# Eleven projections in a feed-forward, its normalisation moved to ScalarE, and two pairs of attention scores interleaved

## The chip, the cores and the metric

The kernel runs on one core of a Trainium2 chip. The metric is the device time of one execution in microseconds (us). The engines are named TensorE (PE; PEld is its weight load), VectorE (DVE), ScalarE (ACT), GpSimd (POOL) and SyncE (SP).

## The reference, cut to what matters

Eight items of 512 tokens with 256 channels pass through two layers. What the change touches:

```
# layer 0, branch "ffn" (two depths), for each item
h = shift_token(x)                    # second half of the channels one token later
x = x + local_attention(h) @ wo       # window 128, 8 heads
h = shift_token(x)
h = (h - mean(h)) / sqrt(var(h) + 1e-5) * lg + lb
a, g = split(h @ w1 + b1)             # 682 columns each
x = x + (a * gelu(g)) @ w2 + b2
# layer 1, branch "attn": causal latent attention, 16 heads, scores over 24 of 32 rows
# layer 1, branch "ffn": 8 experts, the best 2 of each token; rows are scattered to experts
```

Beside the feed-forward branch of depth 0, layer 0 has a retention branch for the same item.

## The kernel before, in words

The program is a chain of stages k = -1 to 15, written out by hand for every engine. Stages 0 to 7 are the items at depth 0, each beside the retention of the same item; I call them retention stages. Stages 8 to 15 are the items at depth 1, each beside the latent attention (item b = k - 8). In stages 9 to 15 the second half of the latent attention of item b - 1 is also done ("behind"); stage 15 is the last one and has no next item. After it comes the loop over 71 expert tiles.

A stage has three parts. First a loop over four token tiles t: the q/k product (four matmuls) and the v product (two) of the next item, the retention or latent work between them, and on VectorE and GpSimd the rotary parts (L1655, L1657), their sum (L1497), the sums of squares (L1661) and the power (L1501). Then the loop over the feed-forward's chunks c = 0 to 5. Then a loop over u with the local attention of the next item.

PSUM is used as two rings of four banks of 512 columns. Ring A is emptied mostly by ScalarE, ring D by VectorE. The names that take two banks are q/k, its transposes, the scores and a few more. A product waits until the jobs that were last in its banks are emptied; the order of the jobs is written out in ring_a_jobs and ring_d_jobs, and every engine works through its instructions in that order.

The feed-forward: shifted_stats (L1631, L1633) takes mean and variance of each tile of the shifted input, which SyncE puts together by small DMAs (L566 to L570). GpSimd makes rs, the power -1/2 (L1466). shifted_apply on VectorE runs ln_apply (L1641) in eight instructions of 128x128 at t = 1 (in the last stage t = 2). TensorE turns z (L733), ScalarE applies lg and lb (norm_in, L1254). Chunks are 120 hidden columns wide, the last 82. up_projection makes the gate half in ring A and the value half in ring D (L722), gelu empties the first (L1281), gate_up multiplies (L1717), and down_projection sums over six chunks.

Latent scores: a pair of heads w has three rounds r (ROUNDS): 512, 512 and 256 columns for each head, two banks each. latent_scores issues a pair's heads in two groups of 32 rows (L878). clipped moves each round to the space of the pair on VectorE (L1775), latent_exp (L1307) runs on ScalarE when all three are there, and causal (L1513, L1514, L1516) masks on GpSimd. latent_values of group g (L888) waits for the masks of pairs 2g and 2g + 1. by_token turns the result on TensorE (L896) and scales it on VectorE.

At the end of the last stage, counts of rows for each expert are known. SyncE writes rows of zeros behind each expert's region (zero_rows, L627), four before the table is ready and four after the first weights (L643), then waits for all scatters and zeros, and gathers the first rows (L650).

## Time and profile before

| | us |
|---|---|
| three runs, median (lowest, highest) | 2849.97 (2844.25, 2851.5) |
| profiled execution, its own time | 2849.19 |
| its span | 2847.4 |
| TensorE busy | 2703.8 |
| VectorE, ScalarE, GpSimd busy | 1546.2, 1235.8, 1051.0 |

The span is that from the first to the last instruction. Matmuls are pipelined and their ends are modelled, so the pitch from one group to the next tells more than the busy time of one. A time in square brackets behind a row is how long the engine had been idle, with what ended it.

### The profile page before, as it was taken

How to read it: one execution, taken by the hardware profiler on the slowest of the kernel's cores; microseconds unless marked ns; L12 is line 12 of the kernel's file. 1: busy time of each engine (PE TensorE's matmuls, PEld its weight loads, DVE VectorE, ACT ScalarE, POOL GpSimd, SP SyncE). 2: the span in 40 equal slices, each digit the busy share in tenths (PEclk: the TensorE clock that was granted, in tenths of full speed). 3: DMA queues.
4: the chain of work that ended last, by engine and by line, in shares of the span. 5: the costliest groups of instructions: out<-in, count | busy, mean ns of one | idle time of the engine just before them, and what ended most of it. 6: DMA issues, size and time to landing. Idle time of an engine off the chain costs nothing.

```text
span 2847.4 us, 41985 instructions
## 1 busy us (share of the span) xinstructions
PE 2703.8 (95%) x15582; PEld 1833.3 (64%) x15582; DVE 1546.2 (54%) x3730; ACT 1235.8 (43%) x2287; POOL 1051.0 (37%) x726
## 2 busy tenths in 40 slices
PE   6999999999999999999999999999997799999993
PEld 4575757566575757555555555555564578999993
DVE  6565566575666555677676767576855322100004
ACT  4454444545453444545454545454543234222222
POOL 5434243443434243445454536363623122111110
PEclk9999999999999999999999999999998899999997
DMA  4000000000001001101010101010000666899987
GB/s 143 12 16 26 26 16 30 27 27 16 26 16 57 18 24 52 61 5 53 4 53 5 53 4 45 12 39 19 30 34 23 235 247 250 304 365 365 360 334 243
DMA packets 85907, 261.83 MB, mean 92 GB/s; under 512 B 10668, under 2 KB 49916, under 8 KB 67020
## 3 DMA queue, kind: packets, MB, share of 16 engines
q1 hardware_dynamic: 75004, 237.19, 23.0%
q0 software_dynamic: 6480, 17.77, 1.7%
q10 hardware_dynamic: 4224, 4.19, 0.4%
q8 instruction: 128, 2.10, 0.3%
q14 instruction: 71, 0.58, 0.1%
HBM read 210.81 MB, written 44.11 MB: 90 GB/s over the span
## 4 chain that ended last, share of the span: by engine, by line
PE 65%; issue 13%; DVE 10%; POOL 6%; ACT 3%; DMA 2%; SPq 0%; POOLq 0%; DVEq 0%; ACTq 0%
PE s_pD L722 19%; PE s_pA L722 18%; PE s_pD L878 5%; PE s_pA L772 3%; PE s_pD L794 3%; PE s_pA L781 3%; PE s_pA L1167 2%; PE s_pD L1182 2%; POOL acc_s L1598 2%; DVE s_qk L1676 2%; POOL s_rinv L1501 2%; PE s_pA L761 1%; DMA s_z<-s_cur 1%; PE s_pA L733 1%; PE s_pA L888 1%
## 5 line engine op out<-in xcount | busy, mean ns | idle before, releaser
L1507 POOL TENSOR_TENSOR s_qk<-s_qk,s_rrec 128x1024 f32<-128x1024 f32 (+1 forms) x128 | 220.7, 1725 | 502.7 <-DVE s_rrec L1682 502.5
L722 PE MATMUL s_pA<-s_w_wqkv,s_curT 128*128 128x512 f32 x768 | 354.6, 602 | 5.6 <-ACT s_curT L1212 3.7
L1236 ACT ACTIVATE s_qk<-s_qk,s_mx 128x256 f32<-128x256 f32 (+1 forms) x512 | 239.8, 471 | 95.3 <-DVE s_mx L1676 95.3
L1775 DVE TENSOR_SCALAR s_pairs<-s_pD 128x1024 f32<-128x1024 f32 (+1 forms) x192 | 195.0, 1040 | 151.4 <-PE s_pD L878 150.1
L722 PEld LDWEIGHTS s_pA<-s_w_wqkv,s_curT 128*128 128x128 f32 x768 | 142.6, 191 | 176.7 <-issue 163.2
L1501 POOL TENSOR_TENSOR s_rinv<-s_ssq,s_half 128x16 f32<-128x16 f32 x64 | 230.1, 3596 | 59.5 <-DVE s_ssq L1661 59.5
L1598 POOL DMA_INDIRECT acc_s<-s_w_w,s_sq x71 | 68.5, 964 | 470.7 <-ACT s_w_w L1444 463.5
L2139 DVE COPY s_w_wo<-s_pD 128x256 f32<-128x256 f32 x71 | 29.9, 421 | 338.5 <-PE s_pD L1153 338.5
L1466 POOL TENSOR_TENSOR s_rs<-s_ve,s_half 128x4 f32<-128x4 f32 x40 | 42.0, 1050 | 433.4 <-DVE s_ve L1636 433.3
L878 PE MATMUL s_pD<-s_mixer 32*128 32x512 f32 (+3 forms) x1024 | 180.7, 467 | 11.9 <-DVE s_pairs L1775 9.0
L722 PE MATMUL s_pA<-s_zT,s_w_w 128*120 128x512 f32 (+1 forms) x384 | 183.8, 601 | 4.2 <-ACT s_pairs L1281 3.1
L1676 DVE CUSTOM_DVE_ANT_0 s_qk<-s_pA,s_maskw 128x256 f32<-128x256 f32 (+1 forms) x512 | 167.9, 386 | 25.3 <-PE s_pA L772 24.8
L722 PE MATMUL s_pD<-s_zT,s_w_w 128*120 128x512 f32 (+1 forms) x384 | 180.7, 593 | 0.0
L1497 POOL TENSOR_TENSOR s_qk<-s_qk,s_rot 128x1024 f32<-128x1024 f32 x64 | 151.1, 2361 | 51.8 <-DVE s_qk L1657 51.8
L1307 ACT ACTIVATE s_pairs<-s_pairs 128x2560 f32<-128x2560 f32 x64 | 149.7, 2339 | 44.2 <-DVE s_pairs L1775 44.0
L1218 ACT COPY s_qk<-s_pA 128x1024 f32<-128x1024 f32 x64 | 64.8, 1012 | 231.6 <-PE s_pA L722 231.6
L878 PEld LDWEIGHTS s_pD<-s_mixer 32*128 32x128 f32 x1024 | 89.3, 188 | 100.3 <-issue 50.6
L772 PE MATMUL s_pA<-s_qkT 64*128 64x256 f32 (+1 forms) x1024 | 134.2, 380 | 5.7 <-DVE s_mx L1676 3.8
L781 PE MATMUL s_pA<-s_ident,s_qk 128*128 128x128 f32 x896 | 126.9, 282 | 11.4 <-POOL s_qk L1507 6.5
L1665 DVE SCALAR_TENSOR_TENSOR s_qk<-s_rinv,s_qk 128x1024 f32<-128x1024 f32 x64 | 110.9, 1733 | 42.0 <-POOL s_rinv L1501 42.0
L722 PEld LDWEIGHTS s_pD<-s_zT,s_w_w 128*120 128x120 f32 (+1 forms) x384 | 68.6, 179 | 97.1 <-issue 93.1
L1444 ACT ACTIVATE s_w_w<-s_pD,s_w_w 128x256 f32<-128x256 f32 x71 | 33.6, 473 | 219.2 <-PE s_pD L1182 219.2
(268 smaller groups left out, 5724.6 us busy)
## 6 DMA issues: line engine op xcount, KB each, us to landing
s_qkT<-in_m_w SPq DMA_DIRECT2D x48, 1024.0 KB, 6.7
s_v_tm<-in_m_w SPq DMA_DIRECT2D x24, 1024.0 KB, 7.4
s_rot<-in_m_w SPq DMA_DIRECT2D x24, 1024.0 KB, 6.3
s_w_wqkv<-in_m_w SPq DMA_DIRECT2D x23, 1024.0 KB, 7.7
s_qk<-in_m_w SPq DMA_DIRECT2D x23, 1024.0 KB, 5.7
s_w_w<-rows_s SPq DMA_DIRECT2D x71, 129.0 KB, 6.0
s_cur<-in_x SPq DMA_DIRECT2D x8, 512.0 KB, 3.5
xn_s<-s_cur SPq DMA_DIRECT2D x8, 512.0 KB, 2.6
```

The costliest lines, as they stand in the source:

```text
L722: last = nc.tensor.matmul(out, lhs(c), rhs(c), start=(c == 0), stop=(c == n - 1))
L772: last = nc.tensor.matmul(ps[:, place(i) * 256 + lo * P:(place(i) + 1) * 256], qkT[r, h // 2, tile_cols(t)], qkT[r, 4 + h // 2, (t - 1 + l ...
L781: last = nc.tensor.transpose(ps[:, (2 * i + k) * P:(2 * i + k + 1) * P], prob[w % 3][:, i * 256 + k * P:i * 256 + (k + 1) * P], ident[:])
L878: last = nc.tensor.matmul(ps[:, 512 * i + col:512 * i + col + T - kt * P], KT[rows, g % 2, tile_cols(kt)], QT[rows, g % 2, kt * P:T], star ...
L1236: last = nc.scalar.activation(pi, pi, ACT.Exp, scale=-1.0, bias=mx[:, u, i:i + 1], accum_out=rsum[:, u, i:i + 1])
L1307: nc.scalar.activation(ph, ph, ACT.Exp, scale=1.0 / SQ24).then_inc(lexp, 1)
L1497: nc.gpsimd.tensor_tensor(qk[:, t, :], qk[:, t, :], rot[:, t % 2, :], ALU.add)
L1501: nc.gpsimd.tensor_tensor(rinv[:, t, :], ssq[:, t, :], half[:], ALU.pow).then_inc(rinv_rdy, 1)
L1507: nc.gpsimd.tensor_tensor(pi, pi, rrec[:, u, :].unsqueeze(2).broadcast_to((P, 4, 256 - lo)), ALU.mult).then_inc(p_rdy, 1)
L1598: nc.gpsimd.indirect_dma_start(out=S["acc"], out_offset=bass.IndirectOffsetOnAxis(ap=goal[:, w % NX:w % NX + 1], axis=0), in_=m_y[:, w % N ...
L1676: last = nc.vector.tensor_tensor_reduce(out=prob[u % 3][:, h], in0=ps[:, h], in1=maskw[:, lo:256], scale=-1.0, scalar=3e38, op0=ALU.add, o ...
L1775: nc.vector.tensor_scalar(Pl[:, w % SLOTS, :, ROUND_AT[r]:ROUND_AT[r] + ROUND_N[r]], ps[:, :, 0:ROUND_N[r]], 80.0, -80.0, ALU.min, ALU.max ...
```

## The change

1. The feed-forward's 682 hidden columns are split into 42 + 5 x 128 instead of 5 x 120 + 82. The small chunk is now the first. Its value half and its gate half (from column 64 on) stand side by side in w1, so one projection of 106 columns in ring D makes both; the job in ring A falls away. GELU of chunk 0 reads ring D. The memset for the row of ones moves from chunk 5 to chunk 0.
2. The normalisation of the shifted input: VectorE makes shift = -mean * rs in one small instruction, and ScalarE applies scale and shift in eight, after its copies of t = 1.
3. In stages 9 to 14 the scores of pairs 4 and 5 are issued by four_scores, round by round for both pairs, in four groups of 32 rows: round 0 before the q/k product of tile 0, round 1 before its v product, round 2 at tile 1. The clips, exponentials and masks follow in a new order.
4. The zeros for experts 4 to 7 are written from ScalarE's queue in the last stage instead of SyncE's.

```diff
-HCH = 120
+HCH = 128
-HSZ = [min(HCH, HID - HCH * c) for c in range(NHC)]
+HSZ = [HID - HCH * (NHC - 1)] + [HCH] * (NHC - 1)
+GATE = 64
...
 def up_projection(b, c):
-    ps = slotA("g", b, c)
-    project(ps[0:n, 0:T], ... HID + c * HCH ...).then_inc(mmA, 1)
+    n = HCH if c else GATE + HSZ[0]
+    if c:
+        ps = slotA("g", b, c)
+        project(ps, ...).then_inc(mmA, 1)
     ps = slotD("a", b, c)
...
+def four_scores(b, g, r):
+    pe.wait_ge(outD, doneD["lq", b, g])
+    ps = [slotD("sc", b, 2 * g + pr, r) for pr in range(2)]
+    last = {}
+    for kt, col in ROUNDS[r]:
+        for h in range(4):
+            rows = slice(32 * h, 32 * h + 32)
+            i = h % 2
+            last[h] = nc.tensor.matmul(ps[h // 2][:, 512 * i + col:512 * i + col + T - kt * P], KT[rows, g % 2, tile_cols(kt)],
+                                       QT[rows, g % 2, kt * P:T], start=True, stop=True)
+    last[1].then_inc(mmD, 1)
+    last[3].then_inc(mmD, 1)
...
 # TensorE, loop over t
-    if s.behind and t < 3:
+    if s.behind and (s.last and t < 3 or t == 2):
         latent_scores(b - 1, 4 + t, (0, 1))
+    if s.behind and not s.last and t < 2:
+        four_scores(b - 1, 2, 2 * t)
     if s.ahead:
         qk_product(k + 1, t)
...
-    if s.behind and t < 3:
+    if s.behind and (s.last and t < 3 or t == 2):
         latent_scores(b - 1, 4 + t, (2,))
+    if s.behind and not s.last and t == 0:
+        four_scores(b - 1, 2, 1)
     if s.ahead:
         v_product(k + 1, t)
...
 # ScalarE
+def shifted_norm(b):
+    act.wait_ge(shift_h, b + 1)
+    for t in range(NT):
+        for i, ap in enumerate((cur[b % 2][:, t, 0:P], hB[:, t, :])):
+            last = nc.scalar.activation(z[:, t, i * P:(i + 1) * P], ap, ACT.Identity, bias=shift[:, t:t + 1], scale=rs[:, t:t + 1])
+        last.then_inc(norm_h, 1)
...
+    if s.here and t == 1:
+        shifted_norm(k)
-    if s.behind and t < 2:
+    if s.last and t < 2:
         latent_exp(b - 1, 4 + t)
+    if s.behind and not s.last and t in (1, 2):
+        latent_exp(b - 1, 3 + t)
...
+    if s.last and u == 5:
+        act.wait_ge(zero_rdy, 2)
+        act.wait_ge(weight_rdy, TOPK * LAST + 1)
+        for e in range(E // 2, E):
+            n = act.value_load(counts_i[0:1, e:e + 1], min_val=0, max_val=B * T)
+            act.dma_start(S["rows"][bass.ds(n + e * REG, P), :], zrows).then_inc(zero_in, 16)
...
 # GpSimd, ahead of rotary_sum and head_norms of tile t
-    if s.behind and t < (2 if s.last else 3):
+    if s.last and t < 2:
         causal(b - 1, 4 + t)
+    if s.behind and not s.last and t:
+        causal(b - 1, 3 + t)
...
 # VectorE
 def shifted_apply(b):
     dve.wait_ge(rstd_h, b + 1)
-    for t in range(NT):
-        ln_apply(t, halves(b, t), z, norm_h)
+    nc.vector.scalar_tensor_tensor(out=shift[:], in0=mv[:, :, 0], scalar=-1.0, in1=rs[:], op0=ALU.mult, op1=ALU.mult).then_inc(shift_h, 1)
...
+    if s.behind and not s.last and t < 2:
+        clipped(b - 1, 4, (2 * t,))
+        clipped(b - 1, 5, (2 * t,))
     if s.here and t == 0:
         shifted_stats(k, range(0, 2) if s.last else range(0, NT))
...
+    if s.behind and not s.last and t == 0:
+        clipped(b - 1, 4, (1,))
+        clipped(b - 1, 5, (1,))
```

## Rows read from the trace of the kernel before

**Rows 1.** The page, part 1: busy time of each engine.
```profile
PE 2703.8 (95%) x15582; PEld 1833.3 (64%) x15582; DVE 1546.2 (54%) x3730; ACT 1235.8 (43%) x2287; POOL 1051.0 (37%) x726
```

**Rows 2.** Groups by line (busy us, mean ns, idle before), a half of the normalisation.
```profile
L1641 DVE SCALAR_TENSOR_TENSOR s_z<-s_z,s_mv,s_rs 128x128 f32<-128x128 f32 x64 | 23.7, 371 | 0.0
```

**Rows 3.** Timeline (start us, us) of retention stage 4.
```profile
626.10 0.34 DVE L1641 SCALAR_TENSOR_TENSOR s_z<-s_cur,s_mv,s_rs 128x128 f32<-128x128 f32 x1
...
628.32 1.01 ACT L1218 COPY s_qk<-s_pA 128x1024 f32<-128x1024 f32 x1 [6.30 <-PE s_pA L722]
...
650.47 1.88 PE L722 MATMUL s_pA<-s_zT,s_w_w 128*120 128x512 f32 x4
...
653.90 1.04 PE L761 MATMUL s_pA<-s_ident,s_qk 128*128 128x128 f32 x8
```

**Rows 4.** Timeline of latent stage 12, scores of pairs 4 and 5.
```profile
1686.82 1.99 PE L878 MATMUL s_pD<-s_mixer 32*128 32x512 f32 x12
...
1688.07 2.36 DVE L1775 TENSOR_SCALAR s_pairs<-s_pD 128x1024 f32<-128x1024 f32 x2 [2.15 <-PE s_pD L878]
...
1688.75 3.70 PE L722 MATMUL s_pA<-s_w_wqkv,s_curT 128*128 128x512 f32 x8
...
1692.38 0.70 PE L878 MATMUL s_pD<-s_mixer 32*128 32x256 f32 x4
...
1695.48 0.29 DVE L1631 BATCH_NORM_STATS2 s_stat<-s_cur 128x6 f32<-128x128 f32 x1 [2.35 <-DMA s_z<-s_cur]
...
1696.32 3.15 DVE L1775 TENSOR_SCALAR s_pairs<-s_pD 128x512 f32<-128x512 f32 x3
...
1704.22 0.60 PE L896 MATMUL s_pD<-s_ident,s_mixer 128*128 128x128 f32 x4
```

**Rows 5.** Timeline of latent stage 12, from the exponential of pair 5 on.
```profile
1704.90 2.34 ACT L1307 ACTIVATE s_pairs<-s_pairs 128x2560 f32<-128x2560 f32 x1
...
1710.59 1.73 POOL L1516 TENSOR_TENSOR s_pairs<-s_pairs,s_tri 128x512 f32<-128x512 f32 x1
...
1714.20 2.35 POOL L1497 TENSOR_TENSOR s_qk<-s_qk,s_rot 128x1024 f32<-128x1024 f32 x1 [1.89 <-DVE s_qk L1657]
...
1716.51 3.90 POOL L1501 TENSOR_TENSOR s_rinv<-s_ssq,s_half 128x16 f32<-128x16 f32 x1
...
1719.00 2.36 PE L888 MATMUL s_pA<-s_pairs,s_mixer 128*32 128x512 f32 x32
...
1740.83 2.36 PE L888 MATMUL s_pA<-s_pairs,s_mixer 128*32 128x512 f32 x32 [0.65 <-POOL s_pairs L1516]
...
1743.58 1.41 DVE L1717 SCALAR_TENSOR_TENSOR s_pairs<-s_pD,s_w_b,s_pairs 120x512 f32<-120x512 f32 x2
...
1745.17 1.98 PE L722 MATMUL s_pA<-s_zT,s_w_w 128*120 128x512 f32 x4 [0.51 <-ACT s_pairs L1281]
```

**Rows 6.** Instructions of line L1294 (ns min/median/max), a normalisation ScalarE already does.
```profile
L1294 ACT ACTIVATE s_mixer<-s_mixer,s_shift,s_rs x28: 585/587/602, 1195.7 to 2069.9; 128x256 f32<-128x256 f32 x28
```

**Rows 7.** Windows: stretch, busy of PE, PEld, DVE, ACT, POOL, granted clock, DMA.
```profile
1190.00:1195.00 5.00, 2.61 (x24) 1.87 (x24) 4.68 (x14) 2.90 (x9) 1.28 (x3) 1.00 0.58 208
1195.00:1200.00 5.00, 4.24 (x19) 3.39 (x20) 2.73 (x16) 4.28 (x13) 3.76 (x4) 0.51 0.01 3
```

**Rows 8.** Timeline of TensorE: stage 8 (two places) and stage 15.
```profile
1141.94 0.67 PE L722 MATMUL s_pA<-s_w_wqkv,s_curT 128*128 128x512 f32 x1 [0.36 <-ACT s_sq L1221]
...
1195.76 1.65 PE L772 MATMUL s_pA<-s_qkT 64*128 64x256 f32 x6 [3.15 <-DVE s_mx L1676]
...
2150.33 3.77 PE L722 MATMUL s_pA<-s_zT,s_w_w 128*120 128x512 f32 x4 [1.11 <-ACT s_zT L1254]
```

**Rows 9.** Timeline of the queues of SyncE and GpSimd before the expert tiles.
```profile
2223.25 4.29 SPq L627 DMA_DIRECT2D rows_s<-s_w_fC  x4
2223.53 0.96 POOL L1527 DMA_INDIRECT rows_s<-s_w_w,s_rows_i  x1 [0.30 <-issue]
...
2232.87 0.36 SPq L650 DMA_DIRECT2D s_w_w<-rows_s  x1
```

More of the change, by code:

```diff
@@ L26 @@
 HID = 682
-HCH = 120
+HCH = 128
 NHC = 6
-HSZ = [min(HCH, HID - HCH * c) for c in range(NHC)]
+HSZ = [HID - HCH * (NHC - 1)] + [HCH] * (NHC - 1)
+HAT = [0] + [HSZ[0] + HCH * c for c in range(NHC - 1)]
+GATE = 64
+ONES = 32
+UPW = GATE + HSZ[0] + 2 * HCH * (NHC - 1)
 LH, LDH, LDR, LAT = 16, 16, 8, 64
@@ L119, in ring_a_jobs @@
         for c in range(NHC):
-            if s.here:
+            if s.here and c:
                 j += [("g", k, c)]
@@ L170, in ring_d_jobs @@
         for t in range(NT):
-            if s.behind and t < 3:
+            if s.behind and (s.last and t < 3 or t == 2):
                 j += pair(b - 1, 4 + t)
+            if s.behind and not s.last and t < 2:
+                j += [("sc", b - 1, 4 + i, r) for r in ((0, 1) if t == 0 else (2,)) for i in range(2)]
             if s.ret:
@@ L624, in _ @@
             sp.dma_start(S["rows"][E * REG:E * REG + P, :], zrows).then_inc(zero_in, 16)
-            def zero_rows(e):
+            for e in range(E // 2):
                 n = sp.value_load(counts_i[0:1, e:e + 1], min_val=0, max_val=B * T)
                 sp.dma_start(S["rows"][bass.ds(n + e * REG, P), :], zrows).then_inc(zero_in, 16)
-            for e in range(E // 2):
-                zero_rows(e)
             sp.wait_ge(table, 1)
@@ L644, in fetch @@
                 if u == 0:
-                    for z in range(E // 2, E):
-                        zero_rows(z)
                     for k in range(TOPK):
@@ L1004, in _ @@
                         ret_products(k, t)
-                    if s.behind and t < 3:
+                    if s.behind and (s.last and t < 3 or t == 2):
                         latent_scores(b - 1, 4 + t, (2,))
+                    if s.behind and not s.last and t == 0:
+                        four_scores(b - 1, 2, 1)
                     if s.ahead:
@@ L1277, in gelu @@
                 n = HSZ[c]
-                ps = takeA("g", b, c)
+                at = 0 if c else GATE
+                if c:
+                    ps = takeA("g", b, c)
+                else:
+                    act.wait_ge(mmD, DJ["a", b, 0] + 1)
+                    ps = pD[:, colsD[DJ["a", b, 0]]]
                 if b > 0 or c >= 2:
                     act.wait_ge(outD, doneD["a", b, c - 2] if c >= 2 else doneD["a", b - 1, NHC - 1])
-                nc.scalar.activation(gl_of(b)[c % 2][0:n], ps[0:n, 0:T], ACT.Gelu, bias=W["b1"][0:n, 1, c:c + 1]).then_inc(outA, 1)
+                last = nc.scalar.activation(gl_of(b)[c % 2][0:n], ps[at:at + n, 0:T], ACT.Gelu, bias=W["b1"][at:at + n, 1, c:c + 1])
+                last.then_inc(outA if c else first_gelu, 1)
             def final_tanh(b, i):
@@ L1970, in _ @@
                 for t in range(NT):
-                    if s.behind and t < 3:
+                    if s.behind and (s.last and t < 3 or t == 2):
                         clipped(b - 1, 4 + t, (0, 1))
+                    if s.behind and not s.last and t < 2:
+                        clipped(b - 1, 4, (2 * t,))
+                        clipped(b - 1, 5, (2 * t,))
                     if s.here and t == 0:
@@ L1979, in _ @@
                         ret_rotary(k, t)
-                    if s.behind and t < 3:
+                    if s.behind and (s.last and t < 3 or t == 2):
                         clipped(b - 1, 4 + t, (2,))
+                    if s.behind and not s.last and t == 0:
+                        clipped(b - 1, 4, (1,))
+                        clipped(b - 1, 5, (1,))
                     if s.past and t == 1:
@@ L2217, in arrange @@
     r["w_ln"] = np.stack([np.stack([per(g), per(b)], 1) for g, b in zip(a["L0_ffn_ln_g"], a["L0_ffn_ln_b"])], 1)
-    r["w_w1"] = np.stack([ch(w) for w in a["L0_ffn_w1"]], 1)
+    up = []
+    for c in range(NHC):
+        value = a["L0_ffn_w1"][:, :, HAT[c]:HAT[c] + HSZ[c]]
+        gate = a["L0_ffn_w1"][:, :, HID + HAT[c]:HID + HAT[c] + HSZ[c]]
+        room = np.zeros(value.shape[:2] + (0 if c else GATE - HSZ[0],), np.float32)
+        up += [value, room, gate]
+    r["w_w1"] = np.stack([ch(w) for w in np.concatenate(up, 2)], 1)
     b1 = np.zeros((HCH, DEPTH, 2, NHC), np.float32)
@@ L2224, in arrange @@
             for i in range(2):
[L2225 to L2227 removed]
+                at = 0 if c or not i else GATE
+                b1[at:at + n, l, i, c] = a["L0_ffn_b1"][l, i * HID + HAT[c]:i * HID + HAT[c] + n]
+            w2[0:n, l, c] = a["L0_ffn_w2"][l, HAT[c]:HAT[c] + n]
+        w2[HSZ[0], l, 0] = a["L0_ffn_b2"][l]
     r["w_b1"], r["w_w2"] = b1, w2
```

23 lines of the change are left out of this document (12 added, 11 removed).

## The prediction

> **What bounds the kernel now.** I read the busy times first, then the groups by line, then the timeline of one stage of each kind. The reader is to see in the first which engine is full, in the second what the moved instructions cost where they are, and in the last which wait ends last. TensorE is busy for 2703.8 of 2847.4 us [rows 1]; in the retention stages (0 to 7) it hardly ever waits, and each of the latent stages 9 to 14 holds a few waits of at most 1 us. So an instruction taken off TensorE is worth its own pitch, as long as no other engine moves into its place; work taken off VectorE is worth nothing unless TensorE waited for it.
>
> **The feed-forward in eleven projections.** Each of the twelve 512-column projections of an item is two matmuls, which the trace shows as four records [rows 3]. The gate and value projections of chunk 0 fill TensorE from 650.47 to 653.90, so one costs 1.72 us [rows 3]. The width of a chunk (120, 82 or now 128 columns of weights) does not show in that pitch, and the down projection keeps its six chunks. Taken out once in each item: -1.72 us. In the eight retention stages nothing waits for it, since VectorE idles there before its first product: 8 x 1.72 = -13.8 us. The memset that moves to chunk 0 (0.5 us, VectorE) and the later first GELU lie inside that idle time.
>
> **The normalisation on ScalarE.** VectorE loses eight instructions of about 0.34 us an item and keeps one small one [rows 2]. ScalarE gains eight. The nearest row is its own 128x256 Identity with scale and bias by row, 585 ns [rows 6]; at half the columns I take 0.38 us each, 3.0 us for eight (bounds 2.4 and 4.0). They stand after the copies of t=1, so everything behind them on ScalarE waits until VectorE reaches its step. In a retention stage VectorE gets there at 626.10 and the next copy starts at 628.32 [rows 3]: it would be 1 us late, which the retention branch's projections between two uses of those banks cover. I cost it at nothing; without that cover it is the 1.1 us of stage 8. In stage 8 that cover is gone, and TensorE already waits 0.36 us for the square behind the copy [rows 8]: +1.1, which leaves -0.6 for that stage.
>
> **The scores of pairs 4 and 5, stages 9 to 14.** This decides. Now the first two rounds of pair 4 take 1.93 us (1686.82 to 1688.75) and its third 0.63; two row groups run side by side [rows 4]. With four side by side, both pairs need 1.06 + 1.06 + 0.65 = 2.8 us instead of twice 2.56. But a round then fills all four banks of the D ring, so the next round needs both clips before it. VectorE's order is: both clips of round 0, the statistics of all four tiles, both clips of round 1. The last tile's statistics wait for a DMA until 1695.48 whatever TensorE does, and the first clip after them starts at 1696.32 [rows 4]. Two clips take 2.36 (1688.07), so these end at 1698.7. By my count TensorE has done round 0, q/k product, round 1 and v product at 1694.5, and waits 4.3 us. Then 0.65 + 3.64 + 1.85 us bring it to the turn by token at 1704.95; before, that began at 1704.22 [rows 4]. The whole saving in the scores is gone: +0.7 us at this point (bounds: -2.3 if the statistics end early enough, +1.5).
>
> The Trainium skill, TensorEngine Tiling (Array Packing), section PSUM Bottleneck, says that tiling speeds up TensorE but not the emptying of PSUM, which may become the limit after a fourfold speed-up. The trace agrees as far as it goes: two clips of together 2.36 us do not fit beside a v product of 1.85, so by that rule alone, without the DMA, the third round would wait 0.5 us and not 4.3, and 1.8 us of the gain would be left.
>
> **What is late next.** The exponential of pair 5 began at 1704.90 before, that of pair 4 one tile earlier [rows 5]. Now ScalarE first waits for the shift, which VectorE makes only after the turn by token (about 1706.5), spends 3.0 us on the rows, and then takes 2.34 for pair 4: 1711.9. GpSimd's order now puts the mask of pair 5 behind the rotary sum and the power of tile 1: mask 4 (three instructions that end with the row at 1710.59, 2.65 to 3.1 us), sum 2.35, power 3.9, mask 5 again 2.65 [rows 5]. That ends at 1723.5. TensorE would want the values of that group at about 1720.4 (it did at 1719.00 before [rows 5]): a second wait of some 3.1 us, +4.5 in all against before (bounds +2.5 and +5.5). The copy of q/k tile 2 behind the exponential costs 0.5 of this.
>
> After that TensorE saves its 1.72, and it had waits of 0.65 and 0.51 us of its own (1740.83, 1745.17), which can absorb some of the rest: +1.6 there if TensorE is the limit. But the gate product that frees the GELU (1743.58) hangs on VectorE's clips of pair 7, the rotary parts of tile 3, GpSimd's power and the router's chain, all behind the same wait: +4.1 if they are the limit [rows 5]. I take +3.1 a stage. The shorter queue on VectorE is in this.
>
> **The clock.** A gap of 3.15 us before 1195.76 [rows 8] is followed by five microseconds at 0.51 of the clock, and then more [rows 7]: the lower level, 1.2 GHz. It means for four records of a projection 3.77 us (at 2150.33) instead of 1.88 [rows 8, 3]. So a wait of 4.3 us is likely to cost a stretch at half rate, and one of 3.1 us may. A dense stretch of 3.4 to 6.8 us at half rate loses 1.7 to 3.4 us. I take 2.5 for both waits of a stage together (bounds 0 and 6.8, two stretches of each size). The Trainium skill, TensorE: Matmul & The Clock Gate, section Why this matters for your kernels, warns of the same: a pause between bursts of matmuls brings back the lower rate.
>
> Latent stages: 6 x (3.1 + 2.5) = +33.6 us.
>
> **The last stage and the turn to the experts.** In stage 15 the normalisation itself may get faster, but exponential 5 now stands between it and the copies, so I count nothing for it. The projection that is removed ran at the half clock (3.77 us [rows 8]) and the next at nearly the full one: between 1.72 and 3.4, I take -2.4. At the end SyncE issued four rows of zeros from 2223.25 for 4.3 us after the first weights; the first gather, on which TensorE waits, went out at 2232.87 [rows 9]. Moved to ScalarE, they go out before those weights; behind them on ScalarE stand only two copies whose products TensorE can make while it waits. What is late next is the last scatter, issued at 2223.53 by GpSimd [rows 9] and, as I estimate, landed by 2230: -2.8 (bounds 0 and -4).
>
> **The sum.** -13.8 - 0.6 - 2.4 - 2.8 = -19.6; with +33.6 it is +14.0. The profiled execution took 2849.2 us (span 2847.4 and 1.8 around it), 0.8 below the median of the three runs. That gives 2863. About 0.3%, 8.5 us, is what a measurement of this kernel can tell from no change.
>
> **The rivals.**
> - The gain arrives (0.27): VectorE's statistics and the masks are not what TensorE meets, for instance because the values of the group come late enough for GpSimd, and only the first wait is left. The place is the turn by token and the values behind it. A stage then ends at +0.7 + 0.5 - 1.72 = -0.5; 6 x -0.5 - 19.6 = -22.6: 2827. It decides from the point where mask 5 ends before TensorE wants it, 3.1 us earlier than I count. For it: rows of GpSimd's power differ by up to 1 us, and the ScalarE time is estimated. Against it: four instructions in series on one engine, each with its row.
> - The waits come but the clock holds (0.22): 6 x 3.1 - 19.6 = -1.0: 2848. For it: gaps of 1 to 2 us elsewhere leave the clock at 1.00. Against it: the first wait is longer than the gap of 3.15 us.
> - The four row groups do not run side by side (0.09): the change would not do what it says. No row shows four of them. A round of both pairs takes 1.93 instead of 1.06, mostly out of the first wait, and the third 0.4 more; the first wait shrinks to 2.6 us and the clock probably holds: 6 x 3.5 - 19.6 = +1.4: 2851.
> - Both waits bring long stretches at half rate (0.07): 6 x (3.1 + 6.8) - 19.6 = +39.8: 2889.
>
> The forecast has 0.35. Cases of both signs hold most of the chance; the forecast's own range is 2855 to 2874, by the bounds of the two waits. The whole range, 2824 to 2879, reaches to the rival that gains and leaves out the worst clock. Slower by over 0.3%: the forecast's 0.35 less a little, the long half rates and a tenth of the others: 0.46. Within: 0.25. Faster: 0.29.
>
> **What would show it.** In a latent stage of the changed kernel: TensorE idle some 4 us before the third round, ended by the clip L1775; some 3 us before the values (L888), ended by GpSimd's mask L1516; granted clock near 0.5 after them. Row groups: four records of round 0 starting together, and 1.06 us for its eight. Retention stages shorter by 1.7 us each. The first gather 3 us nearer to the table. Latent stages no longer than before would prove the forecast wrong; retention stages that do not shrink would take its other half.

## The result, and the profile after

The changed kernel takes 2892.81 us (median of 4 runs, 2891.88 to 2893.25) against 2850.73 (4 runs, 2844.25 to 2852.95) in the same session: 1.015 of the time before, 95% interval 1.0136 to 1.0164. It is 42 us slower; the forecast was 2863 with a range to 2879. The profiled execution has a span of 2890.1 against 2847.4 us.

The head of its profile page, which answers to [rows 1]:

```profile
span 2890.1 us, 41880 instructions
PE 2705.3 (94%) x15518; PEld 1817.5 (63%) x15518; DVE 1488.9 (52%) x3618; ACT 1287.8 (45%) x2415; POOL 1032.9 (36%) x726
```

TensorE has 64 fewer matmul records (two for each of 32 matmuls) and yet is busy for 1.5 us longer; VectorE lost 57 us of work. Neither says where the time went. For that I cut both traces at the first addition of each stage (L1695 before, L1742 after) and compared lengths. What each stage gained (-) or lost (+), us, by this cut:

| stage | 0 to 7 | 8 | 9 | 10 | 11 | 12 | 13 | 14 | 15 to the end |
|---|---|---|---|---|---|---|---|---|---|
| after - before | -0.5 each | +2.6 | +7.2 | +8.4 | +9.5 | +5.7 | +9.5 | +7.7 | -3.5 |

Before stage 0 it is -0.3. The latent stages 9 to 14 hold +48.0. Windows of the changed kernel over stages 4, 8 and 12 (PEclk is the mean granted clock):

```profile
core 0: us, PE busy (x) PEld busy (x) DVE busy (x) ACT busy (x) POOL busy (x), PEclk, DMA share, GB/s
600.77:729.51 128.74, 127.93 (x686) 81.86 (x684) 77.48 (x194) 63.86 (x136) 49.83 (x27) 1.00 0.07 23
1112.82:1242.28 129.46, 122.40 (x637) 76.28 (x636) 74.81 (x168) 65.43 (x129) 51.78 (x32) 0.96 0.11 37
1703.45:1855.68 152.23, 140.23 (x813) 82.25 (x812) 97.63 (x226) 78.30 (x137) 69.84 (x51) 0.98 0.08 27
```

Stage 12, TensorE's timeline where the forecast had its two waits (compare [rows 4, 5]):

```profile
1710.14 1.14 PE L895 MATMUL s_pD<-s_mixer 32*128 32x512 f32 x8
1711.21 3.70 PE L725 MATMUL s_pA<-s_w_wqkv,s_curT 128*128 128x512 f32 x8
1714.85 1.15 PE L895 MATMUL s_pD<-s_mixer 32*128 32x384 f32 x16
1715.92 1.98 PE L725 MATMUL s_pA<-s_w_wqkv,s_curT 128*128 128x512 f32 x4
1722.29 0.71 PE L895 MATMUL s_pD<-s_mixer 32*128 32x256 f32 x8 [4.39 <-DVE s_pairs L1823]
1722.94 7.11 PE L725 MATMUL s_pA<-s_w_wqkv,s_curT 128*128 128x512 f32 x12
...
1750.20 4.05 PE L906 MATMUL s_pA<-s_pairs,s_mixer 128*32 128x512 f32 x32 [5.13 <-POOL s_pairs L1561]
```

Three things are to be seen. The four row groups work: round 0 of both pairs, four matmuls of 512 columns in eight records, takes 1.07 us to the next start (1710.14 to 1711.21), where one pair's first two rounds took 1.93. Then TensorE waits 4.39 us for clips and 5.13 us for mask 5; all six latent stages have both waits, 4.39 to 4.45 and 5.12 to 5.13. And behind each wait the work is slow: the twelve records from 1722.94 take 7.11 us instead of 5.4, in part in a stretch at 1.2 GHz (granted clock 0.51):

```profile
1722.90:1726.30 3.40, 3.40 (x8) 1.51 (x5) 3.16 (x5) 0.00 (x0) 0.00 (x0) 0.51 0.01 2
```

VectorE in the first wait: the clips of round 1 (L1823) start when the statistics of the last tile are done, and these waited for a DMA.

```profile
1718.95 0.29 DVE L1678 BATCH_NORM_STATS2 s_stat<-s_cur 128x6 f32<-128x128 f32 x1 [2.35 <-DMA s_z<-s_cur]
...
1719.79 2.35 DVE L1823 TENSOR_SCALAR s_pairs<-s_pD 128x1024 f32<-128x1024 f32 x2
```

ScalarE (first two rows) and GpSimd in the second wait, which answers to [rows 5]: the last of eight norms, exponential 4, mask 4, sum, power, mask 5.

```profile
1734.07 0.48 ACT L1277 ACTIVATE s_z<-s_z,s_shift,s_rs 128x128 f32<-128x128 f32 x1
1734.45 2.32 ACT L1342 ACTIVATE s_pairs<-s_pairs 128x2560 f32<-128x2560 f32 x1
```

```profile
1736.85 0.73 POOL L1558 TENSOR_TENSOR s_pairs<-s_pairs,s_tri 128x256 f32<-128x256 f32 x1 [4.70 <-ACT s_pairs L1342]
...
1738.22 2.26 POOL L1561 TENSOR_TENSOR s_pairs<-s_pairs,s_tri 128x512 f32<-128x512 f32 x1
1740.45 2.80 POOL L1542 TENSOR_TENSOR s_qk<-s_qk,s_rot 128x1024 f32<-128x1024 f32 x1
1743.21 3.36 POOL L1546 TENSOR_TENSOR s_rinv<-s_ssq,s_half 128x16 f32<-128x16 f32 x1
1746.54 0.72 POOL L1558 TENSOR_TENSOR s_pairs<-s_pairs,s_tri 128x256 f32<-128x256 f32 x1
1747.22 1.70 POOL L1559 TENSOR_TENSOR s_pairs<-s_pairs,s_tri 128x256 f32<-128x256 f32 x1
1748.89 1.25 POOL L1561 TENSOR_TENSOR s_pairs<-s_pairs,s_tri 128x512 f32<-128x512 f32 x1
```

Retention stage 4: the merged projection is there, and the down projection has grown. Each of its two groups begins with records of 43 rows. Before, the two groups took 5.38 and 5.19 us; now 5.88 (672.48 to 678.36) and 5.87:

```profile
671.48 1.16 PE L775 MATMUL s_pA<-s_qkT 64*128 64x128 f32 x16
...
672.48 1.68 PE L725 MATMUL s_pD<-s_w_w,s_pairs 43*128 43x256 f32 x6
...
678.36 1.13 PE L775 MATMUL s_pA<-s_qkT 64*128 64x256 f32 x8
679.42 0.65 PE L784 MATMUL s_pA<-s_ident,s_qk 128*128 128x128 f32 x4
680.01 1.76 PE L725 MATMUL s_pD<-s_w_w,s_pairs 43*128 43x256 f32 x6
...
685.88 1.04 PE L736 MATMUL s_pA<-s_ident,s_z 128*128 128x128 f32 x8
```

Summed over both kernels' matmul rows and clock records, the mean latent stage comes out so: TensorE idle 12.4 us instead of 4.6 (+7.8); busy at the half rate 8.7 us instead of 2.3, which costs half of the difference (+3.2); work saved, 2.3 us of scores and 0.5 in the feed-forward (-2.8). That is +8.2, and +8.0 was measured.

Not every stretch at the half rate follows a wait. The kernel before has one of 3.4 us late in four of its six latent stages, and in the 8 us before each TensorE never pauses for more than 0.4 us. In its stage 12 the granted clock is 1.00 while TensorE is busy for all of 7.40 us, the last part with products of 8 columns and of 64 rows, and then 0.50:

```profile
1785.00:1792.40 7.40, 7.40 (x35) 5.03 (x35) 3.05 (x6) 2.18 (x8) 0.00 (x0) 1.00 0.00 0
1792.50:1795.80 3.30, 3.30 (x15) 2.71 (x13) 1.29 (x2) 0.58 (x1) 0.00 (x0) 0.50 0.00 0
```

In the changed kernel one of these four is left. So the stretches at the two waits cost more than the net +3.2: about 4.1 us a stage, less 0.9 for those that are gone.

### The profile page after: what moved, and what is told of

It reads as the page before. It is cut to its first block, busy times and chain, and to the rows that moved or that the text cites. A ratio compares the mean times of both kernels' runs of the same rounds, so it can differ in the third digit from the quotient of the medians.

```text
span 2890.1 us, 41880 instructions
## 1 busy us (share of the span) xinstructions
PE 2705.3 (94%) x15518; PEld 1817.5 (63%) x15518; DVE 1488.9 (52%) x3618; ACT 1287.8 (45%) x2415; POOL 1032.9 (36%) x726
## 4 chain that ended last, share of the span: by engine, by line
PE 61%; issue 14%; DVE 10%; POOL 7%; ACT 4%; DMA 3%; SPq 0%; ACTq 0%; POOLq 0%; DVEq 0%
PE s_pD L725 19%; PE s_pA L725 15%; PE s_pD L883 4%; PE s_pA L775 3%; PE s_pA L784 3%; PE s_pD L797 3%; PE s_pA L1189 2%; PE s_pA L906 2%; PE s_pD L1204 2%; POOL acc_s L1645 2%; POOL s_rinv L1546 1%; DMA s_z<-s_cur 1%; POOL rows_s L1572 1%; PE s_pA L764 1%; DVE s_pairs L1823 1%
## 5 line engine op out<-in xcount | busy, mean ns | idle before, releaser
L725 PE MATMUL s_pA<-s_w_wqkv,s_curT 128*128 128x512 f32 x768 | 366.9, 619 | 7.9 <-ACT s_curT L1234 3.7
L1823 DVE TENSOR_SCALAR s_pairs<-s_pD 128x1024 f32<-128x1024 f32 (+1 forms) x192 | 194.6, 1042 | 204.2 <-PE s_pD L883 182.8
L1546 POOL TENSOR_TENSOR s_rinv<-s_ssq,s_half 128x16 f32<-128x16 f32 x64 | 216.5, 3382 | 86.0 <-DVE s_ssq L1708 86.0
L725 PE MATMUL s_pD<-s_zT,s_w_w 128*128 128x512 f32 (+1 forms) x384 | 182.4, 598 | 2.9 <-ACT s_zT L1283 2.9
L725 PE MATMUL s_pA<-s_zT,s_w_w 128*128 128x512 f32 x320 | 152.4, 599 | 3.1 <-ACT s_pairs L1315 3.1
L883 PE MATMUL s_pD<-s_mixer 32*128 32x256 f32 (+3 forms) x832 | 146.6, 467 | 6.0 <-DVE s_pairs L1823 3.1
L775 PE MATMUL s_pA<-s_qkT 64*128 64x256 f32 (+1 forms) x1024 | 132.3, 378 | 7.4 <-DVE s_mx L1723 3.6
L725 PE MATMUL s_pD<-s_w_w,s_pairs 43*128 43x256 f32 x480 | 137.7, 401 | 0.0
L784 PE MATMUL s_pA<-s_ident,s_qk 128*128 128x128 f32 x896 | 125.8, 280 | 3.5 <-POOL s_qk L1552 2.8
L725 PEld LDWEIGHTS s_pD<-s_zT,s_w_w 128*128 128x128 f32 (+1 forms) x384 | 71.2, 188 | 88.9 <-issue 83.1
```

The lines of the kernel that those rows point to most:

```text
L725: last = nc.tensor.matmul(out, lhs(c), rhs(c), start=(c == 0), stop=(c == n - 1))
L775: last = nc.tensor.matmul(ps[:, place(i) * 256 + lo * P:(place(i) + 1) * 256], qkT[r, h // 2, tile_cols(t)], qkT[r, 4 + h // 2, (t - 1 + l ...
L784: last = nc.tensor.transpose(ps[:, (2 * i + k) * P:(2 * i + k + 1) * P], prob[w % 3][:, i * 256 + k * P:i * 256 + (k + 1) * P], ident[:])
L883: last = nc.tensor.matmul(ps[:, 512 * i + col:512 * i + col + T - kt * P], KT[rows, g % 2, tile_cols(kt)], QT[rows, g % 2, kt * P:T], star ...
L1546: nc.gpsimd.tensor_tensor(rinv[:, t, :], ssq[:, t, :], half[:], ALU.pow).then_inc(rinv_rdy, 1)
L1823: nc.vector.tensor_scalar(Pl[:, w % SLOTS, :, ROUND_AT[r]:ROUND_AT[r] + ROUND_N[r]], ps[:, :, 0:ROUND_N[r]], 80.0, -80.0, ALU.min, ALU.max ...
```

## The experiments

Eighteen kernels ran, sixteen of them timed against the kernel before. The median of the kernel before moved between 2844 and 2851 us from session to session, so ratios are what is compared; across sessions I trust them to about 0.2%, since the changed kernel's 2892.81 came beside 2850.73 and a kernel with stages as long as its own (64 rows, below) took 2892.97 beside 2844.66. "After" is the changed kernel.

**Undoing or mending one part of the change.** The first gives the scores of pairs 4 and 5 their old order on every engine; the second:

```diff
-                rows = [HSZ[c] + (c == 0) for c in range(NHC)]
+                rows = [65 if c == 0 else HCH for c in range(NHC)]
```

The third puts ln_apply back on VectorE. The fourth, on VectorE:

```diff
                         clipped(b - 1, 5, (2 * t,))
+                    if s.behind and not s.last and t == 0:
+                        clipped(b - 1, 4, (1,))
+                        clipped(b - 1, 5, (1,))
                     if s.here and t == 0:
                         shifted_stats(...)
```

> The changed kernel with the score products of pairs 4 and 5 in the order of before on all engines (clips, exponentials and masks with them); merge, norm on ScalarE and zero rows kept. If the two waits of stages 9 to 14 (4.4 and 5.1 us each) with the half-rate stretches behind them are made by the new order of the scores: those six stages lose nearly all of their +48 us, about 2847 (2842 to 2855). If the norm on ScalarE makes the second wait by itself: only the first wait goes, about 2868. If the norm costs the latent stages a little (1 us each) through ScalarE: 2853.

> The changed kernel with chunk 0 of the down projection's sum taken over 65 rows (rows 43 to 64 of the weights are zero) in place of 43; nothing else. If the 43-row products run in a 64-row form of the array and the change of form within each of the four sums costs the 1.2 us by which the two groups of L725 in the down projection grew: groups back at 5.4 and 5.2 us, about 1.2 a stage, sixteen items, 2893 - 19 = 2874 (2866 to 2880). If the growth has another cause (order of the chunks, the buffer's arrival): no change, 2893, or slightly more for a second fill of ones.

> The changed kernel with the shifted input's normalisation back on VectorE, everything else kept. If eight norms ahead of exponential 4 on ScalarE (3.1 us) carry the second wait: it falls from 5.1 to about 2.5 us, stage 8 gives back its +2.6, VectorE pays 0.4 to 0.6 x 8 ahead of its clips; with the clock's stretch in half of the stages 2893 - 20 = 2873 (2862 to 2885). If the place of mask 5 behind sum and power on GpSimd sets that wait alone, and VectorE's norm delays the same chain by as much: 2890 (2887 to 2898).

> The changed kernel with VectorE's two clips of round 1 put ahead of the four tiles' statistics, which wait for transfers; nothing else moved. If the first wait (4.4 us) is these clips held behind the statistics: it falls under 1 us in stages 9 to 14, six times 3.5 to 6 us with the half-rate stretch, 2893 - 25 = 2868 (2858 to 2876). If TensorE's next work waits for the statistics or for the stretch at half rate anyway: under 8 us, 2885 or more.

| run | us | ratio to before (95%) | stage 4 | stage 8 | stages 9 to 14, sum |
|---|---|---|---|---|---|
| after | 2892.81 | 1.015 (1.0136 to 1.0164) | -0.5 | +2.6 | +48.0 |
| scores undone | 2852.69 | 1.0036 (1.0022 to 1.005) | -0.5 | -1.2 | +7.3 |
| 65 rows | 2879.74 | 1.0123 (1.0107 to 1.0138) | -1.7 | +0.6 | +49.0 |
| norm on VectorE | 2883.54 | 1.0146 (1.0131 to 1.0162) | -0.5 | +0.3 | +38.0 |
| clips first | 2870.31 | 1.0091 (1.0076 to 1.0107) | -0.5 | -0.3 | +27.4 |

(The last three columns are stage lengths against the kernel before, from one profile each.) By these profiles the order of the scores made 41 of the 48 us. That is its upper end: the profiled execution of the first run is the fastest of its five (2847.14, median 2852.69), and by the ratios undoing the scores gives back 1.1%, 32 us. The clips alone made the first wait: with them in front it falls from 4.4 to 0.69, and 20.6 us go from these stages. The second wait stays, 5.12:

```profile
1705.49 0.71 PE L895 MATMUL s_pD<-s_mixer 32*128 32x256 f32 x8 [0.69 <-DVE s_pairs L1823]
...
1733.45 4.49 PE L906 MATMUL s_pA<-s_pairs,s_mixer 128*32 128x512 f32 x32 [5.12 <-POOL s_pairs L1561]
```

The norm on ScalarE made 1.7 us of the second wait (3.44 without it) and 2.4 of stage 8's loss. By its ratio the run is hardly faster than after, 1.0146 against 1.015: its profiled execution (span 2877.9) is one of its fastest (timed runs 2879.6 to 2889.41), so the stage sums of that row flatter it.

In the retention stages the 65 rows give back what was missing: every undisturbed one is 1.70 shorter than before, the 1.72 of the forecast. The latent stages gain nothing from them (+49.0 against +48.0): TensorE is idle there for 13.7 us in the mean stage instead of 12.4, so the 1.2 us saved became waiting, and the whole run gained 8 us by the ratios and 13 by the medians, where 19 were expected. The same two groups in stage 4, now 5.38 and 5.18 us:

```profile
666.94 1.16 PE L775 MATMUL s_pA<-s_qkT 64*128 64x128 f32 x16
668.04 1.56 PE L725 MATMUL s_pD<-s_w_w,s_pairs 65*128 65x256 f32 x6
...
673.42 1.14 PE L775 MATMUL s_pA<-s_qkT 64*128 64x256 f32 x8
674.48 0.66 PE L784 MATMUL s_pA<-s_ident,s_qk 128*128 128x128 f32 x4
...
680.16 1.04 PE L736 MATMUL s_pA<-s_ident,s_z 128*128 128x128 f32 x8
```

**Why 43 rows cost 1.2 us.** Two looks. One takes 64 rows. The other keeps 43 and turns the order of the first sum of each group, so that its 43-row chunk comes last and stands beside the 43-row chunk of the second sum:

```diff
+                    at = lambda c: c if k else (c + 1) % NHC
```

> The changed kernel with 64 rows instead of 43 in chunk 0 of the down projection (65 rows gave retention stages of 127.6 us, 43 rows 128.7). If the cost goes with a form of the array for 64 rows or fewer: 128.7. If it goes with the number of rows, 64 and 65 are alike: 127.6.

> The changed kernel (43 rows, chunk 0 first in each sum) with one difference: in the first of the two sums of a group the chunk of 43 rows is taken last, so that it stands next to the 43-row chunk of the second sum. If each change between row counts costs time, the changes in a group fall from four to two and half of the 1.2 us comes back: retention stages 128.1 instead of 128.7 (127.6 with 65 rows). If a 43-row product is slow by itself, wherever it stands: 128.7 as in the changed kernel.

Stage 4 of the run with 64 rows and of the one with 65:

```profile
600.77:729.52 128.75, 127.93 (x686) 81.88 (x684) 77.55 (x193) 63.68 (x136) 49.83 (x27) 1.00 0.07 23
```

```profile
596.24:723.81 127.57, 126.76 (x686) 82.39 (x684) 78.02 (x194) 63.71 (x136) 49.81 (x27) 1.00 0.07 24
```

With 64 rows the stage is as long as with 43 (128.74), with 65 it is 1.18 shorter: the step lies between 64 and 65, and below it the number of rows does not matter. I call the two sides forms of the array. With the order turned the stage takes 128.34, a gain of 0.40 where I expected 0.6 and the rival 0. The rows show why:

```profile
669.74 1.16 PE L775 MATMUL s_pA<-s_qkT 64*128 64x128 f32 x16
...
676.60 1.13 PE L775 MATMUL s_pA<-s_qkT 64*128 64x256 f32 x8
677.66 0.66 PE L784 MATMUL s_pA<-s_ident,s_qk 128*128 128x128 f32 x4
...
683.73 1.04 PE L736 MATMUL s_pA<-s_ident,s_z 128*128 128x128 f32 x8
```

I had not counted the neighbours. The first group stands between products of 64 rows (L775), the second between products of 128 (L784, L736). Count each change between 64 rows or fewer and more, from neighbour to neighbour. First group: 2 with 65 rows, 4 in after, 4 with the order turned. From the start of L775 to the start of the next L775 it takes 6.48, 6.88 and 6.86 us. Second group: 0, 4 and 2 changes; from L784 to L736 5.68, 6.46 and 6.07. Four differences, +0.40 and +0.38 for two more changes, +0.39 for two, +0.78 for four: 0.2 us a change, whatever stands between them. The Trainium skill, TensorEngine Tiling (Array Packing), section Key Properties, says that a change of the tiling mode drains TensorE. The trace agrees, and gives the price here.

**The mended order, and what is left without it.** The next four build on these. The first has clips, exponentials and masks of pairs 4 and 5 in a mended order, with the norm on ScalarE and 43 rows as in after. On ScalarE:

```diff
+                    if s.behind and not s.last and t == 1:
+                        latent_exp(b - 1, 4)
+                        latent_exp(b - 1, 5)
                     if s.here and t == 1:
                         shifted_norm(k)
```

> The changed kernel with four row groups kept but its order mended: VectorE clips round 1 ahead of the statistics, ScalarE takes exponentials 4 and 5 ahead of the eight norms, GpSimd masks 4 and 5 ahead of sum and power of token tile 1, mask 6 stays at tile 3. If the second wait (5.1 us, still there with the clips alone moved) is exponential 4 behind the norms plus mask 5 behind sum and power: it is gone or under 1 us, six times 5.1 plus about 2 for the half-rate stretch behind it below the run with the clips alone (2870): 2870 - 40 = 2830 (2824 to 2842), and the interleaving then gains. If it comes from GpSimd's masks being slow beside VectorE in any order: 2855 to 2868.

> The changed kernel with the scores in the order of before and the normalisation on VectorE, and 65 rows in chunk 0 of the down projection: what is left is the merge and the zero rows. The merge's 1.7 us in the eight retention stages and stage 8 (15.3), about 0.7 in each latent stage (4) and 3.4 behind stage 15: 2844 - 23 = 2821 (2815 to 2828). If the norm on VectorE is what holds the latent stages up: above 2830.

> As the run before it, but with the normalisation kept on ScalarE. The difference of the two is the norm's move alone. If it is free or a small gain, as forecast (stage 8 -0.6, none elsewhere): 2820 (2814 to 2826). If ScalarE is what holds TensorE in the latent stages (its copies of q and k come 3 us late and bring half-rate stretches, as the medians of the run with the scores undone hint, 9 us above before): 2832 (2827 to 2840).

> The changed kernel whole (four row groups, norm on ScalarE, merge, zero rows) with the mended order and 65 rows in chunk 0. If merge and order add up: 1.2 us in each of sixteen stages below the run with the mended order, 2830 - 15 = 2815 (2808 to 2828). If the latent stages hide the merge: 2822.

| run | us | ratio (95%) | stages 9 to 14 |
|---|---|---|---|
| mended order | 2851.8 | 1.0023 (1.0014 to 1.0032) | +9.8 |
| old scores, norm on VectorE, 65 rows | 2838.89 | 0.9979 (0.997 to 0.9988) | +8.4 |
| old scores, norm on ScalarE, 65 rows | 2841.71 | 0.9992 (0.9983 to 1.0001) | +14.0 |
| mended order, norm on ScalarE, 65 rows | 2843.03 | 0.9991 (0.9982 to 1) | +10.8 |

Both waits go, as forecast. Yet none of the four times came in: each was expected 18 to 28 us lower. In the second run, of what the change saves only the retention stages' 1.7 us and the last stage's part arrive; the latent stages are 1.4 us longer than before though they have 1.7 us less to do. In its stage 12 TensorE waits 0.77 us for VectorE's product of chunk 0 and 1.09 for mask 7. In the mended order it does not wait for mask 7 at all, but there is a third wait, for the clips of pair 7, before the merged projection:

```profile
1699.55 0.71 PE L895 MATMUL s_pD<-s_mixer 32*128 32x256 f32 x8 [0.69 <-DVE s_pairs L1827]
...
1715.78 5.39 PE L725 MATMUL s_pA<-s_w_wqkv,s_curT 128*128 128x512 f32 x12 [0.47 <-ACT s_sq L1243]
1730.95 2.96 PE L725 MATMUL s_pD<-s_zT,s_w_w 128*106 128x512 f32 x4 [3.56 <-DVE s_pairs L1827]
```

**Where the latent stages' savings go.** First suspicion: the merged projection goes to ring D, and the gate projection in ring A that used to stand in front covered the clips. I moved the small chunk to third place, with old scores, with four row groups, and with those and the norm on ScalarE.

> Old scores, norm on VectorE, 65 rows, zero rows moved, and the small merged chunk in third place instead of first. With it first, the latent stages gave the merge's 1.7 us back: two new gaps of 0.8 to 1.7 us (before the second value projection, behind VectorE's product of chunk 0, which now waits for a GELU that starts only after the merged projection) and 1.0 before the values of group 3. If the place of the chunk makes them: they go, the latent stages gain 1.5 to 2.5 us each against the run with the chunk first, 2839 - 12 = 2827 (2821 to 2832). If the latent stages are bound by another chain (VectorE and GpSimd into mask 7) that no chunk's place touches: 2836 to 2840.

> As the run before it, with four row groups in the mended order. With the chunk first the mended order had a third wait of 3.6 us before the merged projection, for the clips of pair 7 that free its bank. With a gate projection (the other ring) first, 1.7 us of it are covered: 2843 - 6 x 2 - some of the clock = 2829 (2822 to 2836). If the saved time in the scores (2.3 us a stage) reaches the end at all, it is below the run before it; if VectorE's chain to the clips of pair 7 is the limit, it is level or slower by up to 8.

> As the run before it with the normalisation on ScalarE. VectorE's 3 us of norms a stage are ahead of the clips of pair 7 in the run before it; if those clips are the limit, this is faster by 1 to 2 us a stage: 2829 - 9 = 2820. If ScalarE's wait for the shift holds the copies of q and k by as much: level or up to 4 slower, as with the scores in the old order (2841.7 against 2838.9).

Measured 2842.31 (0.9983, 0.9975 to 0.9992), 2841.05 (0.9981, 0.9972 to 0.999) and 2851.66 (1.0018, 1.001 to 1.0027). The suspicion falls: where the gaps were they go or shrink (the third wait, 3.56 us, to 1.46), and they come back before the values of group 3, 1.74 us in stage 12 of the first and 2.71 in the second, both ended by GpSimd's mask. The third run against the second is the norm alone: 0.4% slower, the opposite of what I expected there. A window of the second, from the first sum on GpSimd to mask 7 in stage 12:

```profile
1690.87:1729.82 38.95, 33.94 (x144) 15.79 (x140) 35.84 (x41) 24.27 (x24) 38.95 (x20) 1.00 0.00 1
```

GpSimd is busy for all of the 38.95 us and VectorE for 35.84. TensorE, at 33.94, is no longer what bounds this part. Part of that busy time is the other engine's doing: the sum at 1703.21 takes 3.35 us on GpSimd, the one at 1709.85 takes 2.34. To tell GpSimd from VectorE I moved the rotary sums of tile 3, then of tiles 2 and 3, to VectorE in these stages (the last of the three runs has the scores in the old order):

```diff
+                if on_vector(b, t):
+                    step(turned)
+                    turned = nc.vector.tensor_tensor(qk[:, t, :], qk[:, t, :], rot[:, t % 2, :], ALU.add)
```

> The run with the small chunk in third place, four row groups in the mended order and the norm on VectorE, and now the rotary sum of token tile 3 (128x1024, 2.4 us on GpSimd) on VectorE in the stages 9 to 14. In that run GpSimd worked without a gap from the first sum to mask 7, 39 us, and TensorE waited 2.7 us for it. If GpSimd's row of sums, powers and masks is what eats the savings in the latent stages: that wait falls by 1 to 2.4 us in each of six stages, 12 below that run, about 0.994 of before, 2829. If VectorE, which now pays 1.1 to 1.6 us for the sum ahead of its products, is as near to the limit: within 3 us of that run.

> As the run before it with the sums of tiles 2 and 3 on VectorE. If GpSimd is still the limit: another 1 us a stage, 2823. If VectorE takes over (it feeds the clips of pair 7 and the products): level with the run before it or up to 6 slower.

> The scores in the order of before, norm on VectorE, small chunk third, 65 rows, and the sums of tiles 2 and 3 on VectorE. With GpSimd relieved, the merge's 1.7 us should come through in the latent stages also: 10 below the run with the small chunk third (0.998 of before), 2831. The difference to the run with four row groups is what the interleaving is worth once GpSimd is not the limit: 2.3 us a stage at most, 14 us; 0 if VectorE's clips are.

Measured 2861.28 (1.0064, 1.0051 to 1.0077), 2851.24 (1.0019, 1.001 to 1.0028) and 2840.41 (0.9986, 0.9978 to 0.9995). With four row groups, relieving GpSimd made it worse, by 0.8% for one sum and 0.4% for two (why one costs more than two stays open); with the old scores two sums changed nothing (0.9986 against 0.9983). VectorE and then GpSimd in stage 12 of the first of these:

```profile
1731.25 2.17 DVE L1717 TENSOR_TENSOR s_qk<-s_qk,s_rot 128x1024 f32<-128x1024 f32 x1
...
1735.22 1.21 DVE L1722 TENSOR_REDUCE s_ssq<-s_sq 128x16 f32<-128x1024 f32 x1
```

```profile
1736.51 3.81 POOL L1553 TENSOR_TENSOR s_rinv<-s_ssq,s_half 128x16 f32<-128x16 f32 x1 [4.17 <-DVE s_ssq L1722]
```

The sum on VectorE delays its products, its clip of pair 7 and its sums of squares, for which the next power on GpSimd then waits 4.17 us. Mask 7 ends 62.7 us after the start of stage 12, where it was 60.8. So GpSimd alone is not the bound: it now has 4 us to spare and the mask is later. That the two engines, which feed each other in this part, bound it together is how I read this; no run relieves both.

**The merge only where it gains.** Last, the small chunk first again, but with a gate projection of its own in stages 9 to 14; old scores, then four row groups in the mended order; norm on VectorE, 65 rows, zero rows moved.

```diff
+def one(k):
+    return not 8 < k < ITEMS - 1
```

> Old scores, norm on VectorE, zero rows moved, 65 rows, and the merge in all stages but 9 to 14: there the gate of the small chunk has a projection of its own again, in the other ring and first, as before. If the merge itself lengthens the latent stages (it takes away the 1.7 us of matmuls on the other ring that stood in front of the clips of pair 7 and of the first GELU): their +8 goes, 0.9955 of before, 2832. If they are longer for another cause (the small chunk first instead of last, the clock): no change from 0.998, 2839.

> As the run before it with four row groups in the mended order. If VectorE and GpSimd together are the limit between the statistics and mask 7, the interleaving is worth nothing also here: within 3 us of the run before it. If the merge's missing cover hid its gain: up to 8 faster, 2825.

Both took 0.9976 of the time before (2839.32, 0.9966 to 0.9987; 2839.3, 0.9965 to 0.9986). These two beat both kernels, by 7 and by some 50 us; the run with the merge everywhere (0.9979) is not told apart from them. So the merge does not cost the latent stages what I expected (+6.1 without it, +8.4 with it, from one profile each). Of the +6.1, 3.5 is idle time (5.2 us a stage against 4.6) and 1.7 the clock; whether the place of the small chunk makes it was not tried alone. And the interleaving is worth nothing: TensorE is idle for 8.0 us in the mean latent stage with it and 5.2 without, which is the 2.3 us of matmuls saved and a little more. Two pairs of runs above say the same, 0.9983 and 0.9981 with the small chunk third, 0.9992 and 0.9991 with the norm on ScalarE.

## Why the prediction was wrong, point by point

**Right.** The sign, and the mechanism of both waits: place, releaser and the row that holds them. The first was forecast at 4.3 and measured at 4.4. Row groups: 1.06 us forecast, 1.07 measured. With the DMA out of the way (clips first) the third round waits 0.69 us. The Trainium skill's rule on emptying PSUM (TensorEngine Tiling (Array Packing), section PSUM Bottleneck), weighed in the forecast, had made that 0.5. The up projection's 1.72: the 65-row run shows 1.70 in every undisturbed retention stage.

**The feed-forward: "the down projection keeps its six chunks".** This step failed. It keeps the number, but its smallest chunk went from 83 rows to 43, below the step at 65: six changes of form more in an item, 0.2 us each. Such changes stood in the trace of before (L878 beside L722 in [rows 4]), and I gave them no price. I read the pitch of the up projection, where the number of columns doesn't show, and used it for the rows of another product. The eight retention stages gave 4.2 us and not 13.8: 9.6 of the miss of 30.

**The second wait: 5.13, not 3.1.** A mis-sized term. I took 2.65 us for a mask; beside a busy VectorE both masks took about 3.6 (1736.85 to 1740.45, 1746.54 to 1750.11), which is the 2 us. The eight norms took 3.1, as counted. Counted from the stage's start, exponential 4 ended 1.5 us later than forecast, but TensorE came for the values 1.4 later too, so that part cancels. (On the way to 1704.95 the forecast's own terms add up to 1704.8, which changes nothing.) Idle time and saved work make +5.0 of a latent stage (7.8 - 2.8) where the forecast had +3.1. In this sum 1.2 is the down projection, but the run with 65 rows shows that taking it away only lengthens the waits.

**The clock: 2.5 a stage, measured 3.2 net, 4.1 for the two waits.** A mis-sized term too. Each wait is followed by a stretch of 3.4 or 6.8 us; of the longer ones part lies inside the wait and costs nothing. What one stretch costs is seen in the 65-row run: stage 6 has one of 3.4 us and is 1.6 us longer than its neighbours. So +5.6 became +8.0 for a latent stage: 14 more of the miss. The rival that came nearest in its total, 2889 with long half rates, was so for the wrong reason: it put 9.9 us on a latent stage, 6.8 of them on the clock, and took the retention stages' gain whole.

**Stage 8: -0.6 forecast, +2.6 measured.** ScalarE's copies were late, as forecast, but by 1.8 us and not 1.1 (the gap of 0.36 in [rows 8] became 2.16); later gaps of the stage shrank by 0.5. The half rate, to which I gave no price there, took 2.0 more than before, most of it in a stretch behind that gap, and the merge gave 0.5. With the norm on VectorE the stage is +0.3. With the clips first and the norm kept it is -0.3, though the gap is still 2.15: there no half rate follows it, so the clock decides here too.

```profile
1139.30 7.07 PE L725 MATMUL s_pA<-s_w_wqkv,s_curT 128*128 128x512 f32 x12 [2.16 <-ACT s_sq L1243]
```

**"The normalisation ... I cost it at nothing".** That holds in the retention stages: with it and without it they are equal to 0.02 us. In stages 8 to 14 it costs 0.4% with the new scores and the small chunk third. With the old scores it is 0.13% (2838.89 and 2841.71), with intervals that overlap, so hardly told from nothing.

**The last stage: -5.2 forecast, -3.5 measured.** The wait for the first gather fell from 7.85 us to 1.70:

```profile
2278.72 0.41 PE L1175 MATMUL s_pD<-s_ident,s_w_w 128*128 128x128 f32 x2 [1.70 <-DMA s_w_w<-rows_s]
```

Most of that is TensorE arriving later and not the rows arriving earlier. From the start of stage 15 to this row it was 118.4 us and is 115.9. In between, the 43-row down projection took 12.0 us instead of 10.64, both at a granted clock of 1.00, and two later products ran longer at the half rate (3.70 us became 6.65, 5.38 became 6.24). The zero rows alone were not tried by themselves.

**The rival that gains (2827).** It named the right condition, mask 5 in time. But meeting it did not give the gain: in the run with the mended order the latent stages are +9.8 and not -3. I had said of the kernel before that a matmul taken off TensorE is worth its own pitch. That holds in the retention stages. In the latent stages TensorE had the highest busy share and short waits, but VectorE and GpSimd, chained through clip, power and mask, stood right behind it, and what was saved came back as waiting for one of them: for the clips of pair 7, for VectorE's product of chunk 0 or for mask 7. That it comes back is shown, for the merge, for the 65 rows and for the four row groups. That the chain of the two engines is the reason is read from the waits and one window, and it is not shown which change to them would let the savings through.

## What to carry to other kernels

When a product is cut anew, look at every product that uses the same cut: a chunk that falls to 64 rows or fewer puts changes of form into a sum of larger ones, 0.2 us each here, and a row of zeros more is the cure. Before interleaving, write down who empties the banks and what that engine does next: a clip behind an instruction that waits for a DMA turned 2.3 us saved into 4.4 us of waiting, and moving two lines gave 20 us back. And an engine with the highest busy share need not be the bound if two others pass work back and forth behind it: add up their part of the stage before pricing what is taken off the first.

## What the runs showed of the hardware

- A change of TensorE between products of 64 rows or fewer and products of more costs 0.2 us (four differences of 0.38 to 0.78 us for two or four changes), and the step lies between 64 and 65 rows (stage 4, 128.75 and 127.57).
- A stretch at the lower clock is not always the price of a wait: stage 12 of the kernel before falls to 0.50 at 1792.5 us after 7.4 us without a pause, and a gap of 2.2 us in stage 8 was followed by a stretch in the changed kernel but not in the run with the clips first.
- VectorE and GpSimd stretch each other in some pairs of instructions and not in others. Two rotary products of 128x512 take 1.28 us on VectorE while GpSimd idles, and one of 128x1024 takes 1.22. Beside the end of mask 4 and the sum on GpSimd the first two took 1.76 and 2.84; beside the power the third took 1.22 as before. One by one:

```profile
1733.93 1.28 DVE L1702 TENSOR_TENSOR s_rot<-s_qk,s_w_fS 128x512 f32<-128x512 f32 x2
1735.25 1.22 DVE L1704 TENSOR_TENSOR s_qk<-s_qk,s_w_fC 128x1024 f32<-128x1024 f32 x1
...
1739.28 1.76 DVE L1702 TENSOR_TENSOR s_rot<-s_qk,s_w_fS 128x512 f32<-128x512 f32 x1
1740.96 2.84 DVE L1702 TENSOR_TENSOR s_rot<-s_qk,s_w_fS 128x512 f32<-128x512 f32 x1
1743.83 1.22 DVE L1704 TENSOR_TENSOR s_qk<-s_qk,s_w_fC 128x1024 f32<-128x1024 f32 x1
```

The row at 1739.28 ends 0.56 us after GpSimd's mask (1738.22 and 2.26), the one at 1740.96 ends 0.55 after GpSimd's sum (1740.45 and 2.80), as if each had begun only then. The Trainium skill, SBUF — State Buffer, section SBUF: two separate sides, calls the port pair of VectorE and GpSimd an exclusive lock held for a whole instruction, where VectorE reads two inputs from SBUF and GpSimd reads SBUF too. The rows beside mask and sum fit that; the product beside the power, which also reads two, does not. What moves the power itself between 2.92 and 3.90 us is not shown. So a duration taken from a row where the other engine idled can be a lower bound only, and for the two masks this was the step that cut the second wait short.
